# One own-key session per batch, four batches staged raw, and the output projection over 26 units

## What is computed

```python
q = rmsnorm(x @ Wq.T); k = rmsnorm(x @ Wk.T); v = x @ Wv.T      # per kv head: 4 q heads x 32 rows = 128 rows
q, k = rope(q, pos), rope(k, pos)
kc = k_cache[block_table].reshape(b, 512, HK, D)                # 16 pages of 32 keys per batch
vc = v_cache[block_table].reshape(b, 512, HK, D)
k_all, v_all = concat([kc, k]), concat([vc, v])                 # 512 cached keys and 32 own keys
probs = softmax(where(valid, q @ k_all.T * SCALE, -1e30))
o = probs @ v_all                                               # 64 batches, 8 kv heads
out = o.reshape(b, s, HQ * D) @ Wo                              # 4096 values per row -> 512
```

## Time and profile before

| | us |
|---|---|
| median of 3 runs | 2338.89 (2337.87 to 2340.54) |
| profiled execution, its own time | 2344.05 |
| its span, first to last instruction | 2342.3 |
| TensorE busy | 2287.0 (98%) |
| VectorE busy | 1750.3 (75%) |
| ScalarE busy | 1584.6 (68%) |
| GpSimd busy | 547.0 (23%) |

### The profile page before, as it was taken

How to read it: one execution, slowest core, us unless ns; L and a number is a source line. 1 busy time by engine, 2 the same in 40 slices (tenths; PEclk the granted TensorE clock), 3 DMA queues, 4 the chain that set the end, 5 groups by cost and what they waited for, 6 DMA issues and landing times.

```text
span 2342.3 us, 56743 instructions
## 1 busy us (share of the span) xinstructions
PE 2287.0 (98%) x15392; PEld 2014.4 (86%) x15392; DVE 1750.3 (75%) x5549; ACT 1584.6 (68%) x4381; POOL 547.0 (23%) x712
## 2 busy tenths in 40 slices
PE   8999999999998899999999999999999999999999
PEld 5778888888887799999999999999999999997777
DVE  3434777777778988888878888888888888886332
ACT  4423666665667878878878878878878878875221
POOL 1002444444443121221221221122122122120000
PEclk9999999999999999999999999999999999999999
DMA  4335333333337777777777787787787777774332
GB/s 167 98 104 170 100 100 102 102 106 112 103 95 248 241 240 242 255 249 237 253 246 239 251 255 232 254 257 230 255 256 234 250 253 240 247 237 175 123 129 98
DMA packets 347956, 455.94 MB, mean 195 GB/s; under 512 B 34505, under 2 KB 280841, under 8 KB 343694
## 3 DMA queue, kind: packets, MB, share of 16 engines
q1 hardware_dynamic: 308398, 315.83, 43.1%
q0 software_dynamic: 36864, 134.23, 16.9%
q10 hardware_dynamic: 2528, 4.29, 0.5%
HBM read 374.53 MB, written 79.69 MB: 194 GB/s over the span
## 4 chain that ended last, share of the span: by engine, by line
PE 84%; issue 5%; ACT 4%; DVE 3%; DMA 2%; SPq 2%; POOLq 0%; POOL 0%; ACTq 0%; DVEq 0%
PE oP L1273 15%; PE S L1239 14%; PE S L1196 11%; PE oP L1196 11%; PE S L1292 8%; PE bank L1120 8%; PE bank L1303 7%; PE oP L1120 3%; PE oP L1284 2%; PE oP L1150 2%; DVE k_lo L979 1%; ACT regC L722 1%; SPq L366 1%; ACT oT_hi L735 1%; PE bank L1255 1%
## 5 line engine op out<-in xcount | busy, mean ns | idle before, releaser
L1273 PEld LDWEIGHTS oP<-regC,regK 128*128 128x128 f32 x4096 | 522.7, 192 | 37.6 <-DVE oT_lo L1011 8.7
L1273 PE MATMUL oP<-regC,regK 128*128 128x128 f32 x4096 | 543.2, 276 | 1.3
L994 DVE CUSTOM_DVE_ANT_0 regC<-S,mask 128x544 f32<-128x544 f32 x512 | 368.8, 720 | 144.5 <-issue 144.4
L722 ACT ACTIVATE regC<-regC,nmx 128x544 f32<-128x544 f32 x512 | 385.5, 753 | 9.1 <-DVE nmx L994 8.9
L708 ACT CAST k_hi<-regK 128x544 fp32r<-128x544 f32 x512 | 327.8, 640 | 74.5 <-PE S L1239 67.4
L979 DVE TENSOR_TENSOR k_lo<-regK,k_hi 128x544 fp32r<-128x544 f32 x512 | 368.0, 719 | 4.0 <-ACT k_hi L708 4.0
L549 POOL TENSOR_TENSOR regC<-regC 128x256 f32<-128x256 f32 x320 | 245.2, 786 | 277.9 <-DVE regC L954 277.9
L1120 PE MATMUL bank<-ident,regC 128*128 128x128 f32 x2048 | 307.5, 273 | 1.4 <-ACT regC L770 1.1
L770 ACT COPY regC<-bank 128x512 f32<-128x512 f32 x512 | 297.6, 581 | 2.7 <-PE bank L1120 2.7
L531 POOL DMA_INDIRECT regK<-v_cache,idx x256 | 265.0, 1035 | 87.7 <-issue 87.4
L528 POOL COPY idx<-idx_all 128x4 int32 (+1 forms) x65 | 22.5, 348 | 1106.8 <-PE oP L1284 1005.7
(11 more groups left out here) (138 smaller groups left out, 4307.4 us busy)
## 6 DMA issues: line engine op xcount, KB each, us to landing
regK<-kT_cache SPq DMA_DIRECT2D x1024, 128.0 KB
qkT_d<-regC SPq DMA_DIRECT2D x160, 256.0 KB, 2.3
regC<-qkT_d SPq DMA_DIRECT2D x64, 512.0 KB, 7.7
oT_d<-regC SPq DMA_DIRECT2D x64, 256.0 KB, 6.3
regK<-oT_d SPq DMA_DIRECT2D x16, 1024.0 KB, 4.9
regC<-wqk SPq DMA_DIRECT2D x10, 1024.0 KB, 5.4
v_d<-regC SPq DMA_DIRECT2D x32, 256.0 KB, 2.3
regK<-qkT_d SPq DMA_DIRECT2D x64, 128.0 KB
```

Source lines behind the costliest of these rows:

```text
L722: nc.scalar.activation(p, p, ACT.Exp, bias=nmx[:, u % 4:u % 4 + 1], scale=-1.0, accum_out=rs[:, u % 4:u % 4 + 1]).then_inc(s_exp, 1)
L994: nc.vector.tensor_tensor_reduce(out=p_sb[u % 4], in0=scores, in1=mask[:], scale=-SCALE, scalar=3e38, op0=ALU.add, op1=ALU.min, accum_out= ...
L1273: last = nc.tensor.matmul(oP[:, j * 512:j * 512 + P], v_sb[b][:, m, u % HK * D:(u % HK + 1) * D], pT_sb[u % 2][:, m * P:(m + 1) * P], star ...
```

## The change

- One own-key session per batch, after its eighth unit: two transposes, one copy of 256 columns, eight products with 32 rows. `oP` holds both halves of the heads, 128 columns apart, and is emptied once per batch, in ScalarE's step `u % 8 == 1`, by two copies one after the other (`o_raw`, `o_st`); in that step the K cast stands behind the copy of the turned probabilities.
- All four batches are staged raw (`o_raw` has four buffers) and split in halves of 256 columns each at the units in `HEADS_AT`: ScalarE's part in that unit, VectorE's one unit later. No product waits for a split straight from PSUM.
- The 48 projection products stand in units 4 to 29, two each, one in units 4, 8, 16 and 24. Behind the last group all 48 remain (before, 44).
- The residual of the group before moves from unit 22 to unit 30, so SyncE stores it at k = 3 (before, k = 2), right ahead of the load of the next one into the same buffer, for which it waits until the store has landed.
- The page table is loaded per group in two small buffers (`load_table`, at k = 2), and layer 3's weights `w3` are loaded behind the attention instead of at the start. SyncE's loop holds two groups in one turn. The other engines' loops turn at unit 0.

```diff
-WO_AT = {u: 3 if u in (2, 6, 10, 14) else 2 for u in (UG - 2, UG - 1, *range(20))}
+WO_AT = {u: 1 if u in (4, 8, 16, 24) else 2 for u in range(4, 30)}
...
+HEADS_AT = {1: (1, 3, 0), 5: (1, 0, 1), 7: (1, 1, 1), 9: (1, 2, 1), 11: (1, 3, 1), 19: (0, 0, 0), 21: (0, 1, 0), 27: (0, 2, 0)}
+RESIDUAL = 30
...
+            def load_table(g, par, count):
+
+                sp.dma_start(btab[0:1, par, 0:count],
+                             bt_row[0:1, bass.ds(g * (BT * NPP) + 2 * NPP, count)]).then_inc(s_x2yst, 16)
...
-                    if k == 2 and not first:
+                    if k == 2 and not last:
+                        load_table(g + 1, 1 - par, BT * NPP)
+                    if k == 3 and not first:
                         sp.wait_ge(s_x2y, g)
                         sp.dma_start(x2_d[bass.ds(g - 1, 1)].rearrange("a p n -> p (a n)"), x2r).then_inc(s_x2yst, 16)
                     if k == 3:
-                        ge(sp, s_x2yst, g * 16)
+                        sp.wait_ge(s_x2yst, g * 32 if last else g * 32 + 16)
                         sp.dma_start(x2r, x2_d[bass.ds(g, 1)].rearrange("a p n -> p (a n)")).then_inc(s_x2r, 16)
...
-            with sp.Fori(1, NT - 1) as g:
-                group(g, False, False)
-            group(NT - 1, False, True)
+            with sp.Fori(0, NT // 2 - 1) as gg:
+                group(gg * 2 + 1, 1, False, False)
+                group(gg * 2 + 2, 0, False, False)
+            group(NT - 1, 1, False, True)
...
+            sp.dma_start(w3_sb, w3).then_inc(s_w3, 16)
...
+            def out_heads(g, b):
+
+                act.wait_ge(s_po, g * BT + (b + 1))
+                ge(act, s_lo, g * 8 - 8 + LO_COUNT[b])
+                nc.scalar.copy(o_raw[b].rearrange("p (j r s) -> p j r s", j=4, s=C), o_heads[0]).then_inc(s_oraw, 1)
+                ge(act, s_ostst, g * (16 * BT) + 16 * b)
+                nc.scalar.copy(o_st.rearrange("p (j r s) -> p j r s", j=4, s=C), o_heads[1]).then_inc(s_ost, 1)
...
+                if u % HK == 1 and not (fixed and n == 1):
+                    out_heads(*((g, u // HK - 1) if u > 1 else (g - 1, BT - 1)))
...
-                if u % 4 == 3:
+                if u % HK == HK - 1:
                     turn_own(g, u)
...
+                if h == HK - 1:
+                    pe.wait_ge(s_vs[b], (g * 2 + u // (2 * HK)) * 64 + 64)
+                    pe.wait_ge(s_evB, g * BT + (u // HK + 1))
+
+                    for k in range(2):
+                        for r in range(4):
+                            rows, at = slice(r * C, (r + 1) * C), r * 512 + k * P
+                            last = nc.tensor.matmul(oP[:, at:at + P], vo_sb[b][rows, k * D:(k + 1) * D],
+                                                    pTo_sb[rows, k * P:(k + 1) * P], start=False, stop=(k == 1))
                     last.then_inc(s_po, 1)
```

More of the change, by code:

```diff
@@ L187, in build @@
         k_hi = [parts("k_hi0", KW)]
-        po_sb = [inC(P) for _ in range(2)]
-        pTo_sb = inC(P)
+        pTo_sb = inC(2 * P)
+        po_sb = [inC(P)]
         assert at[0] <= 12 * T
@@ L197, in build @@
         oT_hi, oT_lo = (parts(f"oT_{part}", H2 * P) for part in ("hi", "lo"))
-        o_raw = [inC(T) for _ in range(2)]
+        o_raw = [inC(T) for _ in range(4)]
+        po_sb += [inC(P) for _ in range(3)]
         assert at[0] >= 27 * T
@@ L239, in build @@
         scores = S[:, S0:S0 + KW]
[L241 removed]
+        o_heads = [oP[:, :].rearrange("p (j q r s) -> p j q r s", j=4, q=4, s=C)[:, :, k, :, :] for k in range(2)]
         s_ids, s_const, s_late = sem("s_ids"), sem("s_const"), sem("s_late")
@@ L359, in _, with load_pages @@
                 sp.dma_start(w_raw[j], wqk[j].rearrange("p c n -> p (c n)")).then_inc(s_w, 16)
-            def load_pages(b, par, first=0, count=NPP):
-                _, pages = nc.values_load_multi_w_load_instructions(
-                    btab[0:1, bass.ds(b * NPP + first, count)], engines=SP, min_val=0, max_val=PAGES - 1)
+            def load_table(g, par, count):
+                sp.dma_start(btab[0:1, par, 0:count],
+                             bt_row[0:1, bass.ds(g * (BT * NPP) + 2 * NPP, count)]).then_inc(s_x2yst, 16)
+            def load_pages(table, par, first=0, count=NPP):
+                _, pages = nc.values_load_multi_w_load_instructions(table, engines=SP, min_val=0, max_val=PAGES - 1)
                 for n in range(count):
@@ L423, in _, with group @@
             sp.dma_start(wo_raw, wo[0]).then_inc(s_wo_in, 16)
-            def group(g, first, last):
+            def group(g, par, first, last):
                 for k in range(BT):
@@ L770, in step @@
                 nc.scalar.copy(pT_sb[u % 2], pT).then_inc(s_evA, 1)
-                if u % 4 == 0 and not (fixed and n == 0):
-                    out_heads(g, u)
+                if u % HK == 1 and not (fixed and n + 4 >= NU):
+                    split_k(n + 4, u + 4, g * 2 + (u + 4) // (2 * HK))
                 if u % 4 == 2 and not (fixed and n + 6 >= NU):
                     split_q(g * (UG // 4) + (u // 4 + 2), u + 6, g * 2 + (u + 6) // (2 * HK))
-                if u in LATE_HI:
-                    late_high(g, LATE_HI[u])
+                if u in HEADS_AT:
+                    back, b, half = HEADS_AT[u]
+                    if not (fixed and g < back):
+                        heads_high(g - back, b, half)
             for t in range(NT):
@@ L794, in _ @@
             split_q(1, 4, 0)
-            for u in range(ROT):
+            for u in range(UG):
                 step(0, u)
@@ L798, in _ @@
                     split_wo(0, u - WO_SPLIT, wo_raw)
-            with act.Fori(0, NT - 1) as g:
-                for u in range(ROT, UG):
+            with act.Fori(1, NT - 1) as g:
+                for u in range(UG):
                     step(g, u)
-                for u in range(ROT):
-                    step(g + 1, u)
-            for u in range(ROT, UG):
+            for u in range(UG):
                 step(NT - 1, u)
-            own_turned(NT - 1, UG)
-            out_heads(NT - 1, UG)
+            own_turned(B - 1)
+            out_heads(NT - 1, BT - 1)
+            for u in list(HEADS_AT)[:5]:
+                heads_high(NT - 1, *HEADS_AT[u][1:])
             def high(g, i):
@@ L1044, in step @@
                     split_q(g * (UG // 4) + (u // 4 + 2), u + 5)
-                if u % HK == 4 and u // HK >= 2:
-                    out_low(g, u // HK)
-                if u in LATE_LO:
-                    late_low(g, LATE_LO[u])
-                if before is not None and u == RESIDUAL:
-                    residual(before)
+                if u - 1 in HEADS_AT:
+                    back, b, half = HEADS_AT[u - 1]
+                    if not (fixed and g < back):
+                        heads_low(g - back, b, half, HI_COUNT[b, half])
+                if u == RESIDUAL and not (fixed and g == 0):
+                    residual(g - 1)
             block_qk(0, 0, 0)
@@ L1304, in out_proj, with step @@
                                             start=(i == 0), stop=(i == 3 * H2 - 1))
-                if first + count == 3 * H2:
-                    last.then_inc(s_wo, 1)
-            def step(g, u, before):
+                    if i == 3 * H2 // 2 - 1:
+                        last.then_inc(s_woh, 1)
+                    if i == 3 * H2 - 1:
+                        last.then_inc(s_wo, 1)
+            def step(g, u):
                 n = g * UG + u
@@ L1313, in step @@
                 turn_p(g, u)
-                of = g if u >= UG - 2 else before
-                if u in WO_AT and of is not None:
-                    out_proj(of, WO_FROM[u], WO_AT[u])
+                if u in WO_AT and not (fixed and g == 0):
+                    out_proj(g - 1, WO_FROM[u], WO_AT[u])
                 if u > 0:
```

172 lines of the change are left out of this document (76 added, 96 removed).

## The result

| | before | after |
|---|---|---|
| median of the runs beside each other, us | 2339.72 (2337.87 to 2342.44, 4 runs) | 2407.53 (2405.36 to 2409.36, 4 runs) |
| span of the profiled execution | 2342.3 | 2404.8 |
| mean granted clock of TensorE | 0.995 | 0.975 |

The ratio is 1.0283, with a 95% interval of 1.0271 to 1.0296: the change makes the kernel 2.8% slower, by 68 us. The forecast was 2354 with a range up to 2378. Sign and mechanism were right, the size was far too small, and the time lies outside the range.

The account below looks back on a forecast made before the run. It took TensorE, 98% busy, as the bound, with 3.3 us of waits per 87.20 us group. Gains -46, SyncE loss +57 and tail +4 gave +15 on 2344.05, so 2359; as median 2354, range 2305 to 2378.

Parts of the forecast that it names:

- Part 3: SyncE's queue: waiting for the x2 store, plus loop turns, makes K pages late; loss 57 us, bounds 36 and 72.
- The mechanism: ScalarE's K cast waits for the page DMA once a group from group 2, some 4 us, some 6 with loop turn.
- The store wait: SyncE at the group's end: the x2 store takes 6.6 us to land before the x2 load can issue.
- The first page and the landing: K pages after unit 8 starts: first issued at 0.8 us, landed 16.3; with SyncE's loop turning, 6.0 and 18.3.
- The loop turn: SyncE going round its loop ahead of the pages: 5.2 us more, six times.
- Parts 1 and 2: Single own-key session saves 0.8 us a group; staging and projection spread cut waits from 3.3 to 1.1, saving 2.2.
- Group 0: The first group, without projection and already uneven: gain of 2 us (between 0 and 4).
- The tail: Path from last o to last stage: second copy, x2 store wait, w3 load ahead; +4 us (3 to 5).
- Short store wait: Rival, SyncE's queue: x2 store lands in about 2 us, loss only 20, time 2317; chance 0.17.
- Pages absorb it: Rival, K pages: a later start costs the units nothing, so the gain stands alone, time 2297; chance 0.13.
- Doubled copies: Rival, two copies out of PSUM: next batch's first values lose 0.6 us at all 64 batches, +38, 2392; chance 0.08.
- The fourth: Rival, bare units: waits stay at their rate, own session costs as before, half the gain goes, 2377; chance 0.07.

Follow-up runs that it names:

- filled gap: Changed kernel with unit 15's score products run eight times in each group from 1 on; 2383.64 us, ratio 1.0181 (other chip kind: 2499.13, 1.0109).
- load later: Changed kernel with the load of x2 moved behind the next group's first store of o; 2330.57 us against 2341.35, ratio 0.9948.
- written out: Changed kernel with SyncE's program of the sixteen groups written out, wait for the x2 store kept; 2388.30 us, ratio 1.0196.
- both edits: Changed kernel with x2 load behind the next group's first store of o and SyncE's loop unrolled; 2292.24 us (ratio 0.9776), again 2293.02 (0.9792).
- store late: Kernel before with only the x2 store moved from third to fourth batch, right ahead of the x2 load; 2432.40 us against 2341.35, ratio 1.0388.

## Why the prediction was wrong in size

What failed is the loss of Part 3, 57 us with bounds of 36 and 72: it came to 85 us of gaps and 31 us of slow products behind them, 116. The gaps are TensorE's idle times in units 12 to 16 of the 14 groups from 2 to 15; the slow products are what these units are longer by on top of that.

| step | forecast | measured |
|---|---|---|
| own session, per batch | 1.29 | 1.09 |
| group without a late page | 84.2 | 83.9 |
| gain of all groups | -46 | -56 |
| x2 store waited for | 6.6 | 8.2 |
| loop turn, extra | 5.2 | 3.2 |
| first page after unit 8, without / with turn | 0.8 / 6.0 | 2.8 / 6.4 |
| pages in after unit 8 | 16.3 / 18.3 | 18.4 / 20.3 |
| late from | 13.1 | 13.1 |
| TensorE's gap, 8 and 6 groups | 3.2 / 5.2, sum 57 | 5.3 / 7.2, sum 85 |
| slow products behind the gap | 0 | 31 |
| tail | +4 | +3 |
| span against before | +15 | +63 |

- **The mechanism** held as far as it went. The K cast waits for the page DMA once a group from group 2 on (6.2 to 7.4 us without a loop turn and 8.3 to 9.1 with one, where some 4 and some 6 were forecast), and the version without the waiting store has lost that wait. 13.1 as the point from which a page is late is exact: in group 7 of the changed kernel 20.63 - 7.53, in group 8 18.45 - 5.34, in the version with the load later 17.29 - 4.18.
- **The largest miss was no term of the sum at all.** I costed a stalled TensorE at the length of its gap. Behind each gap the clock was at 1.2 GHz for 6.8 us, of which TensorE worked half or more: 31 us over 14 groups by the steps, 31 by the filled gap. The granted clock of 1.00 in the earlier trace rows was a column that I read and didn't ask what it hung on.
- **The store wait** was mis-sized: 8.2 for 6.6. The 6.6 was set between one store that landed in 5.7 us and one load in 7.1, both from the same stretch, and had no bounds of its own. Over groups 2 to 15 of that trace the load, which stood where the store stands now, behind 16 pages just issued, took 7.0 to 8.3. Behind the wait the traffic is gone, and the x2 load lands in 2.6 us instead of 7.1; the DMA issues of group 7 (KB each, us to landing):

```profile
regC<-x_d SPq DMA_DIRECT2D x1, 256.0 KB, 2.6
```

  The estimate from the Trainium skill (DMA: Bandwidth & Descriptors, Anatomy of one DMA), whose fit is for DMAs that GpSimd issues while these are SyncE's, was 2.6 us for a transfer of this size. The load in the emptied queue agrees with it, the store at 8.2 doesn't.
- **The first page and the landing.** Without a loop turn the pages landed 15.5 us after the first of them was issued, just as forecast (16.3 - 0.8). All of that miss is the first page, at 2.8 instead of 0.8: 1.4 us of it the store wait in these groups, the rest small steps (the ones written in the prediction add up to 21.0 after unit 0, not 21.3). The upper bound of 16.9, which is 0.8 + 16.1, didn't move with the store wait, and the trace passes it by 1.5 us. With a loop turn the first page was nearly right, 6.4 for 6.0, since the longer store wait and the shorter turn cancel, but the pages took 13.8 us instead of 12.3: more was taken off for the gathers being over than the trace gives. From the first page of group 7 to its K cast SyncE's transfers held 58% of the 16 DMA engines and GpSimd's gathers 37%. These steps together are the other 28 us.
- **The loop turn** went the other way, 3.2 for 5.2, since it now stands behind a wait in which the transfers die down. In the version with the load later, with transfers under way, it costs 5.6 to 6.6 again. The rule of the Trainium skill (Runtime: NRT & Kernel Launch, Instruction fetch mechanics), that unrolling avoids the fetch of a branch's target, is borne out: the packet of instructions stands in every turn, written out there is neither the packet nor the gap, and the time falls by 19 and by 38 us.
- **Parts 1 and 2** came out 10 us better. The chain of the trace after, one session under projection (L1269 turn, L1295 values, L1252 next scores):

```profile
1413.11 0.22 PE bank L1269 x2
1413.32 0.75 PE S L1252 x6
...
1415.63 0.66 PE oP L1295 x16
1416.29 0.96 PE S L1252 x6
```

  0.22 + 0.66 + 0.21 = 1.09: the eight products take 0.66, not twice 0.43; I had left that gain to the lower bound. That saves 1.6 us a group instead of 0.8. The waits left are 83.9 - 82.3 = 1.6, not 1.1, so part 2 gives 1.7 for 2.2. Group 0, forecast at -2, is 4.8 shorter in this execution, but took 84.7 to 89.3 in seven executions with the same first group, so that term says little.
- **The tail.** The chain from the last own-key products to the last stage's first product, before and after:

```profile
2132.28 0.48 PE oP L1284 x8
...
2146.74 23.46 PE S L1292 x94
```

```profile
2190.46 0.70 PE oP L1295 x16
...
2191.19 0.59 ACT regC L747
2191.77 0.50 ACT regC L749
...
2192.66 2.50 DMA x_d<-regC
...
2196.08 7.51 DMA regK<-oT_d
...
2209.27 20.89 PE S L1303 x83
```

  Before, 2146.74 - 2132.76 = 14.0; after, 2209.27 - 2191.16 = 18.1: second copy, store wait and w3 as counted, +4.1. The last units ahead of it are 0.9 shorter, which leaves 3.
- **The rivals.** Short store wait, Pages absorb it and Doubled copies are refuted by the traces and by the versions without the wait. The fourth, that the spread does nothing, asked for groups above 85.5 and saw 83.9. Forecast and rivals shared one blind spot: none had a stall cost more than its own length, so the range ended where idle time alone could reach.

## Where the pages land

First page against the start of unit 8, and the K cast's start (or the landing, where it was in time; needed at 11.9, in the kernel before at 12.35), over the versions on the first chip. Left out are group 0, whose first units are uneven, group 1 of the first run with both edits (-6.7, landed 4.6), group 15 of the filled gap (3.0, 19.9) and the version with the projection in units 4 to 23:

| first page, us after unit 8 | pages in | from |
|---|---|---|
| -4.4 to -4.2 | 6.1 to 9.9 | before, store late: groups 1 and 15 |
| -3.4 to -2.3 | 8.7 to 12.4 | both edits; load later without turn; group 1 of all with the change |
| -2.8 to -2.0 | 9.0 to 11.9 | before |
| -1.1 to -1.0 | 13.5 to 15.0 | before, groups 5 and 13 |
| -0.2 | 16.3 | store late, group 15 |
| 0.3 to 1.4 | 17.1 to 17.9 | load later, with turn |
| 1.5 to 3.5 | 16.5 to 19.1 | changed and gap filled without turn, written out, store late |
| 5.2 to 7.0 | 19.2 to 20.6 | changed and gap filled, with turn |

Three microseconds around the start of unit 8 decide over five of landing; GpSimd issues its four gathers from 4.1 us after it, and pages that are not through by then share the 16 DMA engines with them; that this sharing makes the step is argued from the times, no run moved the gathers. The kernel before stood at the edge of this step in all groups, and both edits put it back there.

## What to carry to other kernels

Before a store is moved next to a load into the same buffer, look at what is queued behind the load: the wait costs its length to everything there, and moving the load behind the urgent transfers takes it away at no cost. Price a stall of a busy TensorE at its gap plus the products at half clock behind it, 2.2 us here behind gaps of 3.4 us and more, and don't read a transfer's time off the median of others when it stands behind a burst. An engine whose loop turns right ahead of a deadline is worth writing out: 19 us and 38 us here, the latter once the store wait was gone.

## What the hardware showed that I had not expected

- The granted clock falls to 1.2 GHz behind a single gap of 3.4 to 7.5 us in an otherwise busy TensorE, and stays there for 3.41 or 6.83 us; no gap of that size in the groups of any trace went without. Shorter gaps can do it too. The gaps of 0.96 (kernel before, group 5) and 2.26 us (store late, group 15) had no such stretch behind them; those of 2.22 (gap filled, group 13) and 1.89 us (both edits, group 1) had. On the second chip the filled kernel has 17 gaps of 2.2 to 2.3 us, where TensorE waits for VectorE, and 13 of them are followed by 3.41 us at 1.2 GHz.
- A turn of SyncE's loop takes as long as its packet of instructions does to come, plus some 1.9 us: 3.6 to 4.0 us in all with the transfers died down, 5.7 to 7.4 (kernel before) with them under way.
- The same kernel before takes 2341 and 2342 on two chips and 2471 and 2473 on two others, and what an edit is worth differs with it: writing out SyncE's loop alone gives 3.3% on the slower ones. In the three versions profiled there ScalarE stands still for up to 3.0 us at a time, with a releaser that the trace doesn't name ("remote"), most often ahead of the K cast and of the copy of the turned probabilities, and these waits don't appear on the first chip. Here from the version with both SyncE edits and the projection in units 4 to 23:

```profile
ACT k_hi L728 <- remote: 30.9, 23, 2.0
ACT regC L788 <- remote: 22.6, 24, 1.5
```

  What holds ScalarE there stays open; no trace of the kernel before was taken on those chips.
